# Second cross attention of a two-layer decoder: queries and their biases formed by VectorE in two operations, in place of ScalarE's four

## What is computed

```python
q = split(Q @ Wq + bq)        # Q: layer norm of x; 16 heads of 16 features
k = split(K @ Wk + bk)        # K = V = the context, 375 tokens per sequence
v = split(V @ Wv + bv)
scores = jnp.einsum('bhsd,bhtd->bhst', q, k) / jnp.sqrt(jnp.float32(d))
scores = jnp.where(mask, scores, NEG)
attn = jax.nn.softmax(scores, axis=-1)
out = jnp.einsum('bhst,bhtd->bhsd', attn, v)
return out @ Wo + bo
```

## Time and profile before

| | us |
|---|---|
| median of 3 runs | 1915.1 (1913.19 to 1916.92) |
| the profiled execution's own time | 1915.24 |
| its span in the trace | 1913.9 |
| TensorE busy | 1859.3 (97% of the span) |
| VectorE busy | 1227.0 (64%) |
| ScalarE busy | 720.9 (38%) |
| GpSimd busy | 705.4 (37%) |
| second cross attention, first L1409 to last scores | about 1089 to 1408 |

### The profile page before, as it was taken

The page is one execution under the profiler, slowest core; times in us unless marked ns, Lnnn a source line. Parts: engine busy times, 40 slices in busy tenths (PEclk is TensorE's granted clock), DMA queues, the critical chain, the costliest instruction groups (busy, mean ns, idle before and its releaser), DMA issues.

```text
span 1913.9 us, 40450 instructions
## 1 busy us (share of the span) xinstructions
PE 1859.3 (97%) x15176; PEld 1361.8 (71%) x15176; DVE 1227.0 (64%) x3332; ACT 720.9 (38%) x1819; POOL 705.4 (37%) x728
## 2 busy tenths in 40 slices
PE   7699999999999999999999999999999999999999
PEld 4477777777776666666445766666659979889698
DVE  6888888889866676777766766666655334234332
ACT  4234444444444555554000365655542212121221
POOL 5634443444205666666000266666634000000000
PEclk9899999999999999999999999999999999999999
DMA  6211211121203010100000000000030000000000
GB/s 186 31 27 24 35 19 29 27 30 16 28 17 124 25 37 25 36 26 20 1 1 1 10 20 21 29 20 28 12 155 23 1 10 1 10 1 1 10 1 10
DMA packets 126080, 53.85 MB, mean 28 GB/s; under 512 B 108744, under 2 KB 117824, under 8 KB 125120
## 3 DMA queue, kind: packets, MB, share of 16 engines
q1 hardware_dynamic: 125888, 51.27, 10.8%
HBM read 45.38 MB, written 5.85 MB: 27 GB/s over the span
## 4 chain that ended last, share of the span: by engine, by line
PE 86%; DVE 7%; issue 3%; ACT 1%; SPq 1%; POOL 1%; DMA 1%; DVEq 0%; ACTq 0%; POOLq 0%
PE ps L2528 18%; PE ps L560 8%; PE ps L1514 6%; PE ps L1536 5%; PE ps L2400 5%; PE ps L2062 5%; PE ps L1552 4%; PE ps L1591 4%; PE ps L1570 4%; PE ps L626 3%; PE ps L2604 3%; PE ps L692 2%; PE ps L1657 2%; PE ps L1523 2%; PE ps L1602 1%
## 5 line engine op out<-in xcount | busy, mean ns | idle before, releaser
L1975 POOL TENSOR_TENSOR h_w<-h_w 125x336 int32<-125x336 int32 x384 | 336.2, 904 | 211.8 <-ACT h_w L1756 211.7
L1860 DVE CUSTOM_DVE_ANT_0 h_w<-ps,h_w 112x375 f32<-112x375 f32 x512 | 263.5, 544 | 1.1 <-issue 0.8
L907 DVE SCALAR_TENSOR_TENSOR big_b<-ps,taps,big_b 128x444 f32<-128x444 f32 (+2 forms) x288 | 194.1, 674 | 21.4 <-ACT big_b L802 6.4
L1756 ACT ACTIVATE h_w<-ps 125x336 f32<-125x336 f32 x512 | 197.7, 468 | 22.4 <-PE ps L1536 22.4
L273 POOL TENSOR_TENSOR rstd<-var_eps,minus_half 112x4 f32<-112x4 f32 x12 | 12.2, 1016 | 406.9 <-DVE var_eps L260 406.9
L1536 PEld LDWEIGHTS ps<-h_w 32*125 32x125 f32 x3072 | 96.6, 184 | 62.3 <-issue 61.5
L1536 PE MATMUL ps<-h_w 32*125 32x112 f32 x3072 | 118.7, 283 | 8.0 <-DVE h_w L1860 5.4
L1869 DVE TENSOR_TENSOR h_w<-h_w,ps 128x112 f32<-128x112 f32 x128 | 34.7, 271 | 141.7 <-PE ps L1523 141.7
L1514 PE MATMUL ps<-h_w 32*112 32x375 f32 x1024 | 121.1, 519 | 0.8 <-DVE h_w L1860 0.8
L2062 PE MATMUL ps<-expert_w,big_a 128*112 128x512 f32 x256 | 113.6, 595 | 0.0
L560 PE MATMUL ps<-h_w,kq_w 128*128 128x448 f32 x256 | 110.7, 556 | 0.0
(11 more groups left out here) (352 smaller groups left out, 3962.7 us busy)
## 6 DMA issues: line engine op xcount, KB each, us to landing
h_w<-in_h SPq DMA_DIRECT2D x2, 4096.0 KB, 16.6
kq_w<-in_ctxT SPq DMA_DIRECT2D x16, 375.0 KB, 3.1
h_w<-in_ctxT SPq DMA_DIRECT2D x16, 375.0 KB, 3.1
h_w<-in_mask SPq DMA_DIRECT2D x16, 164.1 KB, 3.3
kq_w<-in_kq_w SPq DMA_DIRECT2D x8, 256.0 KB, 3.4
w<-in_vz_w SPq DMA_DIRECT2D x8, 256.0 KB, 3.6
blocks<-h_w SPq DMA_DIRECT2D x128, 12.2 KB
expert_w<-in_expert_w SPq DMA_DIRECT2D x1, 2048.0 KB
```

The source lines that it names most:

```text
L907: dve.scalar_tensor_tensor(p3(dst)[:, :, i:], p3(ps[:, bank, 0:GT])[:, :, 0:T - i], k.taps[:, h, n, TAPS - 1 - i:TAPS - i], p3(dst)[:, :, ...
L1756: act.activation(k.PTx[(4 * Q + r) % RING], ps[0:CK, turned_bank(Q, r), 0:NC * T], ACT.Exp).then_inc(s["exp"], 1)
L1860: dve.tensor_tensor_reduce(k.masked[r % 2], ps[0:T, score_bank(Q, r), 0:S2], k.mask_add[n % 2], -1.0, 3.0e38, ALU.add, ALU.min, k.neg_max[ ...
L1975: pool.tensor_tensor(P.bitcast(I32), P.bitcast(I32), k.mask_I[n % 2], ALU.mult).then_inc(s["weights"], 1)
```

## The change

ScalarE no longer forms the queries in the second layer's steps. VectorE does, in a new function `cross_queries_dve`, with two operations, one per `z`, on both halves of the features at once: 224 columns times the factor of the partition, plus a tensor that reads `q_bias` again for each of the 112 tokens. ScalarE waits for `qz` ahead of its copy of the value chunk. The first layer, and sequence 0 of the second, are formed by ScalarE as before.

```diff
+def cross_queries_dve(dve, k, s, seq):
+
+    n = B + seq
+    dve.wait_ge(s["q_proj"], n + 1)
+    dve.wait_ge(s["S"], XH * (n - 1))
+    dve.wait_ge(s["qx"], QUADS * (n - 1))
+    bias = k.q_bias[:, :].rearrange("p (m z) -> p m z", m=KD)
+    for z in range(2):
+        ins = dve.scalar_tensor_tensor(k.Qz[n % 2][:, z, :, :], k.ps[:, 7, 0:KD * T].rearrange("p (m t) -> p m t", m=KD),
+                                       k.q_keep[:, 2 + z:3 + z], bias[:, :, z].unsqueeze(2).to_broadcast([128, KD, T]),
+                                       ALU.mult, ALU.add)
+    ins.then_inc(s["qz"], 1)
...
@@ cross_act, queries(seq)
-        cross_queries_act(act, k, s, l, seq, 7)
+        if l == 0:
+            cross_queries_act(act, k, s, l, seq, 7)
+        else:
+            act.wait_ge(s["qz"], n + 1)
...
@@ cross_dve, in each step, between the mask of the exponentials and the third maximum
+        if l and q == 2 and is_sequence(seq + 1):
+            cross_queries_dve(dve, k, s, seq + 1)
```

## The result

| us | before | changed |
|---|---|---|
| median of 12 runs | 1915.33 (1913.19 to 1917.37) | 1918.43 (1917.42 to 1923.12) |
| the profiled execution's own time | 1915.24 | 1918.27 |
| its span | 1913.9 | 1917.0 |
| VectorE busy | 1227.0 | 1245.7 |
| ScalarE busy | 720.9 | 700.8 |

The changed kernel is slower: the ratio is 1.0021, with a 95% interval of 1.0014 to 1.0029, so 2.7 to 5.6 us on 1915.33. I had forecast 1911.8 and a gain of 3.3. The work did move as planned, 20 us off ScalarE and 19 onto VectorE. The page's part 4 gives the first hint of what it did to the end: VectorE's share of the closing chain rose from 7% to 10%.

A forecast was written before the change was run, and what follows sets the result against it. The prediction took TensorE's own sequence as the bound (86% of the closing chain). Gains of 14 x 0.225 = 3.15 us plus 0.2 in sequence 0 made 3.35, giving 1911.8 us, range 1909.3 to 1914.7.

The forecast's parts named there:

- its worth: TensorE's wait before the second cross attention's output transposes: 0.42 us per sequence, 14 times, 5.9 us at most.
- the pair's price: VectorE's two new query operations: 0.815 us together, from 0.70 at the low end to 1.28 at the high.
- Sequence 0: Second cross attention's first sequence: VectorE is free before the queries are ready; gain 0.2 us (0 to 0.4).
- part 5 (d): VectorE's mask row would begin about when GpSimd's mask does; stretched by 0.48 us, the subtraction L1869 is 0.14 late.
- At nothing: Price put on the work added to VectorE in the second cross attention: no loss, as its delays stay covered.
- (b): VectorE's mask row ends at 1263.78, so L1885 of the normalisation, with 0.92 us idle before, is about 0.04 late.
- C: Slower: the pair is stretched by GpSimd, 0.48 us each; 0.735 lost per sequence, 10.3 us, 1925.4; chance 0.07.
- C stretched once: Milder slower case, the pair stretched by GpSimd only once: 0.255 x 14 = 3.6 us lost, 1918.7.
- A: The wait at the output transposes closes nearly or wholly: 5.0 us gained, 1910.1, or 6.3, 1908.8; chance 0.20.
- B: No gain: pair and late start last as long as ScalarE's four operations, pair 1.035 us, 1915.1; chance 0.08.
- The gain of nothing by the Trainium skill's errata rule: Query operations: two on VectorE 0.72 us, four on ScalarE 0.95; with VectorE's later start, nothing gained.
- If L1639 waits for something else: Sign that would prove the forecast wrong: the output transposes held by something other than ScalarE's value copy.

## Why the prediction was wrong

**Right: the place, its worth and the pair's price.** The wait at the output transposes was the one that the change acts on, 14 times. The pair took 0.80 (0.815 forecast), began where L1896 lets VectorE go, as read, and ScalarE followed it within 0.03. Won per sequence: 0.26, forecast 0.225. Without the collision, the run with GpSimd held back gives a period of 19.90 against 20.15: 14 x 0.25, and with sequence 0's 0.49 (19.40 to 18.91) 4.0 us, where I had a sum of 3.35. Its median lies 4.2 below before. Sequence 0 was undersized, 0.2 against 0.45.

**Wrong: part 5 (d), "At nothing", with (b).** I saw that the mask row would begin with GpSimd's mask (1263.37 and 1263.36) and that it might be stretched. I priced the stretch at 0.48, the difference of L1879's two lengths, and it was 0.68. The larger error was in who waits. I followed VectorE's own order from the row to L1869 and asked what needs L1869, which has over a microsecond of cover. I did not ask who waits for the two instructions in between. The normalisation raises `on`, TensorE's next keys wait for it before they write bank 7, and that wait had no cover. In the kernel before:

```profile
1264.25 0.42 DVE L1889 TENSOR_TENSOR big_b<-ps,inv 112x256 f32<-112x256 f32 x1
1264.70 0.31 PE L1523 MATMUL ps<-ident,h_w 112*128 112x112 f32 x1
1264.93 0.33 PE L1578 MATMUL ps<-ident,h_w 112*125 112x112 f32 x1
```

The normalisation ended at 1264.67 and L1578 began at 1264.93. That distance of 0.26 is the same as in the change, where TensorE plainly waits (1265.32 to 1265.58), so there was nothing to spare in the kernel before either. In the run with the row directly behind the pair, where the distance is 0.35, L1592 starts 0.15 after L1537, and not 0.23 as L1578 here after L1523: the kernel before was already held by some 0.08. The output transposes start at 1263.31 in both kernels' rows, so the rest can be read off directly: the normalisation ended 0.65 later, and TensorE's next transpose began 0.65 later. The rows had the 0.92 of idle time ahead of L1885, and I used it up to 0.04 below nothing without asking what the next user's margin was.

**The rivals.** C had the right mechanism and sign, GpSimd stretching a VectorE operation, and the wrong victim. I looked for it on the pair, where GpSimd was indeed idle, and gave it 0.07. The stretch of the mask row stood in part 5 as a covered detail and should have been a rival with its own price: 0.63 lost less 0.26 won, 14 times. That C stretched once comes to 1918.7, next to the measured 1918.43, is luck: it has the pair stretched, and the output transposes late, and neither happened. A and B did not happen. The gain of nothing by the Trainium skill's errata rule is refuted too: 0.26 were won at the output transposes, and all runs of the changed kernel that avoid the row's collision gain 0.21 or more per sequence, except the one with the values first (0.08), where the displaced row held the normalisation.

**The signs I named.** L1409 left the steady part, 30 new operations of 0.44 us came, L1772's successor came earlier, and the scores waited 0.4 us in all for maxima, as before. The idle time ahead of L1653 fell to 0.09 each, not 0.14, and no engine is named for it. "If L1639 waits for something else" was not it: the wait moved on to the next instruction but two.

## What to carry to other kernels

When work is pushed back on an engine, check every instruction behind it for its own users, not only the one where the engine next idles: a buffer handed back (here bank 7 by the normalisation) is a user like any other. Then check what each pushed instruction will run beside at its new time, on an engine that the trace has shown to hold it up (here GpSimd, which already stretched VectorE's mask of the exponentials in the kernel before). Where two starts would fall within some hundredths of each other, a wait that fixes their order can be worth more than the edit itself: here it turned 0.2% slower into 0.2% faster.

## What the runs showed of the hardware that was not expected

SBUF and PSUM are the two memories that these operations read and write. VectorE's operations from SBUF to SBUF and GpSimd's tensor operations held each other up, and **what had begun first kept its length**. The mask row (375 columns, factor per partition) took 0.41 when it began 0.21 ahead of GpSimd's mask, which then took 0.95 instead of 0.90. It took 1.09 when it began less than 0.02 behind a mask of 0.90, 0.95 when it began 0.16 behind, and 0.68 when 0.43 behind. In all of these it ended 0.21 after that mask did. So it is the rest of GpSimd's operation that counts: with the values first the row began 0.14 before the mask's end and took 0.41, and it was GpSimd's next mask, 0.10 behind it, that took 1.07. The mask of the exponentials (two SBUF inputs) took 0.51 when it began 0.01 ahead of GpSimd's bias addition, which then took 1.07, and 0.98 when it began 0.1 behind, the addition then taking 0.72; it ended 0.37 after the addition. The row maxima, which read one input from PSUM and one from SBUF, stayed at 0.53 to 0.55 beside the same masks.

The Trainium skill, "SBUF — State Buffer", section "Who interferes with whom", states this as a rule: VectorE and GpSimd share one pair of ports, which the first to issue holds for its whole instruction while the other is fully blocked; `tensor_scalar` in a two-port mode and operations with two SBUF inputs use it, those with at most one SBUF input outside these modes do not. The trace agrees on who is stretched and on the order, with the numbers above. The ports, the modes and the full block are not seen in it: the row needs 0.41 alone and ended 0.21 after the mask. By the same rule the pair, with PSUM and one SBUF tensor, was the wrong place to look for rival C. The trace agrees: in the run with the row a step early the pair began 0.43 before the end of GpSimd's bias addition (1256.77 against 1257.20) and took 0.81.
